# The last stage of a two-layer network kernel: time and scale operands built from x columns with one-hot row factors instead of gathered and transposed rows

## Chip, cores and metric

One Trainium2 chip, one of its cores, one program. The metric is the device time of one execution in microseconds (us), the median of the runs shown. Engines are named as in the profile: PE (TensorE), PEld (its weight loads), DVE (VectorE), ACT (ScalarE), POOL (GpSimd), SP (SyncE, here a queue for DMAs).

## What is computed

Only the last part of the reference matters here. `x` is what the attention half and its MLP leave (4 x 1024 tokens, 512 channels), called x1 below. All in fp32:

```
h = ln(x, pw_g[pathway_ids], pw_b[pathway_ids]);  h = ln(h, cp_g[compartment_ids], cp_b[compartment_ids])
t = ln(x, tm_g[time_steps], tm_b[time_steps])
m, n, r = x + one vector per batch each
s = ln(x, ms_g[scale_type], ms_b[scale_type])
cat = concat([w0*h, w1*t, w2*m, w3*n, w4*r, w5*s])
u = ln(silu(cat @ int_W1 + b1) @ int_W2 + b2, int_g, int_be)
q = round and clip u to int8 by its row maximum;  y = (q @ rhs_q) * scales;  out = x + y
```

The layer norm of `t` and `s` is the same for both: x-hat = (x - mean) * rstd per token. Only the gain row differs: one of 5 for `t`, one of 3 for `s`.

## The kernel before

The program runs an attention half, an MLP half and then this last stage, `conditioned_ffn`. The stage works in 8 blocks (b = 0 to 7) of 512 tokens (BT). A block has 16 steps (NS): four for x (all of m, n, r folded into one weight), four for h, and then t and s in turn, one step for each 128 channels (k = 0 to 3): t0, s0, t1, s1 and so on are steps 8 to 15. `main(b, s)` is 12 PE matmuls of 128x512 (four output tiles by three passes, high and low fp32r parts) into the banks A[0..3]; the last four steps are `main_last`, tile by tile (L2112). Then the second layer, `second` (L2133, 48 matmuls), needs the hidden parts: ACT makes silu and the high part (`hidden`, L2361 and L2364), DVE the low part (L2717). The quantised product of the block before, `ff` (L2060), lies between steps 10 and 13.

An operand of a step is made so: its 128 channels by 512 tokens stand as columns in a PSUM bank, ACT copies them as the high part (`front_high`, L2293) and DVE subtracts that for the low part (`front_low`, L2711). For x the columns are loaded from `x1T_d` into `xs` in SBUF. For h, t and s the rows (128 tokens by 512 channels) are turned by four fp32 PE transposes to a bank (`emit`, L2048).

The rows of t and s: POOL gathers a row of 2 x 512 gains for each token (`gather_ts`, L2537, four indirect DMAs a block), DVE multiplies the time half by x-hat (`t_product`, L2701) and POOL the scale half (`scale_rows`, L2544). x-hat in rows is made by ACT from `x1t` (L2302), with scales that DVE and POOL derive from bn_stats (`x_moments`, `rsqrt`, L2548 and L2550).

Nothing is scheduled by a planner. Each engine has a hand-written order, and semaphores between them. `order` is PE's: before `main` of an even step two "items" (turnings) for the steps two ahead, each in one of four ring banks that its predecessor must have left free. In block 0 `first_order` and DVE's `first_steps` take the place, because weights are still being split (`split_low`, `split_second`) and rhs quantised (`rhs_maximum`, `rhs_peak`, `rhs_multiply`, L2992).

POOL's order in a block b (`body`): `scale_rows(b)`, two gathers of h rows for b + 1, the scales of u of block b - 1 (`rsqrt(US)`, L2548), `tail_gain` (eight operations, L2579 and L2581), the scales of x and then the h rows of b + 1 (`tokens`: L2557, L2559, and the gathers L2518 and L2528), the scales of h (`rsqrt(HS)`, ending with L2550), `tail_add` of two tiles (L2587), `gather_ts(b + 1)`, `tail_add` of the other two. ACT's order after step 15 is: h_centre of b + 1 for two tiles, which waits for the scales of h, and only then `hidden(b)`.

SP's order (`tail`): residual loads, for each q tile a DMA transpose (`turn`), the load of x1 rows two blocks ahead, then the stores of the output.

Of the kernel before, what the change touches and what calls it, by code (L numbers as in the profile page):

```python
# [95 lines left out]
def adaln_attn_ffn_kernel(nc, ins, out):  # L96
# [5 lines left out]
    x1T_d = nc.dram_tensor("x1T_d", (D, TOK), F32, kind="Internal").ap().rearrange("(k p) t -> p k t", p=P)  # L102

    ctx = ExitStack()
    with ctx:
# [17 lines left out]
        def following(sems, marks):  # L123
            return mlp_half(nc, at, sems, marks, ps, vec, v, ident, ones_r, eps6, ins, xT, hs2_d, x1_d, x1T_d, p_d, out_v)
# [718 lines left out]
def mlp_half(nc, at, sems, att, ps, vec, v, ident, ones_r, eps6, ins, xT, hs2_d, x1_d, x1T_d, p_d, out_v):  # L843
# [87 lines left out]
    ffn = conditioned_ffn(nc, at, cleared, ps, vec, v, ident, ones_r, ins, x1_d, x1T_d, xt, out_v)  # L931
# [750 lines left out]
def conditioned_ffn(nc, at, cleared, ps, vec, v, ident, ones_r, ins, x1_d, x1T_d, xt, out_v):  # L1682
# [55 lines left out]
    sT = small("states_sb", [P, KT, GROUP])  # L1738
    sel = small("group_sum", [P, GROUP])
# [7 lines left out]
    rstd = small("rstds", [P, 3, TT])  # L1747
    sc = small("token_scale", [P, 3, TT])
    shift = small("mean_shift", [P, 3, TT])
# [35 lines left out]
    cp_rows, ts_rows = sem("f_cp_rows"), sem("f_time_scale_rows")  # L1785
# [39 lines left out]
    T_AT = 0  # L1825
    QT_AT, FF_AT = 8, 10
    QT_STEP = [9, 9, 10, 11]
    ABS_AT, W2_AT, PEAK_AT = 5, 8, QT_AT
    PEAK = {0: 1, 2: 2, 3: 3}

    items = []

    def add_items(s):
        o, k = steps[s]
        items.append((FRONT[o], k, ("op_low", NS, s, 0)))

    order = []
    for s in range(NS):
        if s % 2 == 0 and XF <= s + AHEAD < NS:
# [12 lines left out]
    for n in (0, 4):  # L1852
        at_main = next(i for i, x in enumerate(first_order) if x == ("item", n)) + 2
        first_order.insert(at_main - 2, first_order.pop(at_main))
# [8 lines left out]
    FREED = {2: 1, 3: 2, 6: 3, 7: 4}  # L1863

# [9 lines left out]
    def sync_program(sp, mlp):  # L1874
# [9 lines left out]
        def tail(b, nxt2):  # L1884
# [15 lines left out]
            for t in range(1, TT):  # L1900
                turn(t)
# [11 lines left out]
        def body(b, q, nxt, nxt2):  # L1913
            if nxt:
                sp.wait_ge(S["oh_done"], b + 1)
                load_ids(b + 1)
            if isinstance(b, int) and b == 0:
                sp.wait_ge(S["xh_done"], TT * 2)
                load(2)
            else:  # L1920
                tail(b, nxt2)
# [35 lines left out]
        def early():  # L1957
# [4 lines left out]
            for k in range(2, KT):  # L1962
                sp.dma_start(xs_first[:, k - 2], x1T_d[:, k, bass.ts(0, BT)]).then_inc(first_loaded, 16)
            sp.wait_ge(S["xh_done"], TT)
            load(1)
            sp.wait_ge(tab_zero, 1)
            load_ids(0)

# [4 lines left out]
        def prepare():  # L1973
            sp.wait_ge(ts_rows, 16 * TT)
# [6 lines left out]
            sp.wait_ge(S["op_low"], XF)  # L1981
            sp.dma_start(rows[:].rearrange("p r d -> p (r d)"), ins["rows"]).then_inc(ld["rows"], 16)
# [15 lines left out]
    def tensor_program(pe, mlp, bank_at):  # L1998
        def wait_bank(b, n, prev):
# [7 lines left out]
            while m >= 0 and items[m][0] == "qt" and prev:  # L2007
                m -= len(ring)
            while m >= 0 and items[m][0] in ("qt", "ff") and not prev:
                if items[m][0] == "qt" and items[m][1] in PEAK:  # L2010
                    pe.wait_ge(peak_read, PEAK[items[m][1]])
                    return
                m -= len(ring)
# [14 lines left out]
        def item(b, q, n, prev):  # L2028
# [8 lines left out]
            wait_bank(b, n, prev)  # L2037
            emit(b + off, q if off == 0 else 1 - q, n)

        def emit(b, q, n, dst=None):  # L2040
# [3 lines left out]
            if kind in ("th", "tt", "ts"):  # L2044
                pe.wait_ge(S[{"th": "h_prod", "tt": "t_prod", "ts": "s_prod"}[kind]], TT * (b + 1))
                for t in range(TT):
                    src = {"th": hn[:, t], "tt": gts[t][:, 0], "ts": gts[t][:, 1]}[kind]
                    i = pe.transpose(dst[:, t * P:(t + 1) * P], src[:, k * P:(k + 1) * P], ident[:])  # L2048
# [14 lines left out]
        def peak_item(n, src, ready, count):  # L2063
            wait_bank(0, n, False)
# [5 lines left out]
        def main(b, s):  # L2070
            o, k = steps[s]
            if isinstance(b, int) and b == 0:
# [14 lines left out]
            if s == NS // 2:  # L2087
                if isinstance(b, int) and b == 0:
                    pe.wait_ge(tab_done, 1)
                pe.wait_ge(S["oh_done"], b + 1)  # L2090
                for m in range(KT):
                    rows_m = slice(GROUP * m, GROUP * (m + 1))
                    i = pe.matmul(A[m][:], bias_t[rows_m, :], oh[rows_m, :], start=False, stop=False,  # L2093
                                  tile_position=(GROUP * m, 0))
# [45 lines left out]
        def body(b, q, prev, nxt):  # L2140
            for what, n in order if prev else first_order:
                if what == "main":
                    if n < NS - LG:
                        main(b, n)
                elif prev and items[n][0] == "qt":
                    continue
                elif prev or items[n][0] not in ("qt", "ff"):
                    item(b, q, n, prev)
# [43 lines left out]
        def early(j):  # L2192
# [28 lines left out]
            elif j == 8:  # L2221
                pe.wait_ge(c_chain, 6)
                for k in range(KT):
# [11 lines left out]
            elif j == 10:  # L2235
                pe.wait_ge(b16_done, 4)
# [889 lines left out]
```

## Time and profile before

| | |
|---|---|
| median of 3 runs | 1745.47 us (1743.71 to 1745.48) |
| profiled execution, own time | 1745.17 us |
| its span | 1743.3 us |
| PE busy | 1731.6 us (99%) |
| DVE / ACT / POOL busy | 1192.5 / 875.4 / 789.0 us (68 / 50 / 45%) |
| granted PE clock | 0.999 of full speed |
| last stage | from 1209.6 us to the end, a block takes 64 to 66 us |

A busy PE means here that a matmul is in flight; matmuls are pipelined, so 12 of them whose mean duration reads 389 ns follow one another every 0.23 us. What an engine costs is therefore read from the distance of starts. The span is 1.9 us below the execution's own time; both differ from the median by under 0.3 us apart from that.

### The profile page before, as it was taken

To read this page: it belongs to the slowest core of one execution; us is meant where nothing else is said; L and a number is where in the kernel's file an instruction comes from. 1 tells how busy PE (TensorE), PEld (TensorE's weight loads), DVE (VectorE), ACT (ScalarE), POOL (GpSimd) and SP (SyncE) were. 2 spreads that over 40 slices of the span, in tenths; PEclk is the share of its full clock that TensorE was granted. 3 is DMA by queue.
4 is the path that set the end of the run, shared out by engine and by line. 5 is a ranking of instruction groups with operands and counts; after the bars stand their busy time and mean duration, and the time that the engine had idled before them with its cause. 6 is when DMAs were issued, how large, how long until landed. Compare 5 with 4: busy or idle time off the path is not lost. (4 is left out here: it accounts for less than half of the span.)

```text
span 1743.3 us, 23362 instructions
## 1 busy us (share of the span) xinstructions
PE 1731.6 (99%) x7935; PEld 1408.6 (81%) x7935; DVE 1192.5 (68%) x1756; ACT 875.4 (50%) x1299; POOL 789.0 (45%) x702
## 2 busy tenths in 40 slices
PE   9999999999999999999999999999999999999998
PEld 7888888888888888888888888778887787788786
DVE  7766666669989688785563335357886687577565
ACT  7655556565666665674562223243453443443433
POOL 1122221222686566665560000015577877878742
PEclk9999999999999999999999999999999999999999
DMA  6011100120243334222536568877645445544511
GB/s 208 1 49 49 48 21 27 49 73 25 97 142 121 124 103 163 97 97 89 187 136 224 192 199 283 325 253 244 222 138 180 140 161 174 157 158 151 162 47 61
DMA packets 121992, 234.36 MB, mean 134 GB/s; under 512 B 25619, under 2 KB 25875, under 8 KB 121893
## 3 DMA queue, kind: packets, MB, share of 16 engines
q1 hardware_dynamic: 91732, 157.63, 27.1%
q0 software_dynamic: 11776, 41.95, 7.2%
q10 hardware_dynamic: 18384, 33.56, 5.6%
q8 instruction: 50, 0.82, 0.2%
q14 instruction: 50, 0.40, 0.1%
HBM read 170.71 MB, written 58.72 MB: 132 GB/s over the span
## 5 line engine op out<-in xcount | busy, mean ns | idle before, releaser
L1081 PE MATMUL bank<-h_parts,mlp_w 128*128 128x512 f32 x2016 | 459.3, 389 | 0.6 <-ACT product_copy L1301 0.5
L1081 PEld LDWEIGHTS bank<-h_parts,mlp_w 128*128 128x128 f32 x2016 | 378.1, 188 | 80.4 <-ACT product_copy L1301 1.4
L358 PE MATMUL bank<-h_parts,gate_w 128*128 128x512 f32 x1536 | 351.1, 389 | 0.6 <-DVE h_parts L695 0.6
L358 PEld LDWEIGHTS bank<-h_parts,gate_w 128*128 128x128 f32 x1536 | 288.1, 188 | 61.9 <-issue 0.9
L2085 PE MATMUL bank<-operand_parts,int_w 128*128 128x512 f32 x1152 | 279.0, 395 | 0.1
L1146 PE MATMUL bank<-p_parts,mlp_out_w 128*128 128x512 f32 x1152 | 267.4, 391 | 0.0
L1146 PEld LDWEIGHTS bank<-p_parts,mlp_out_w 128*128 128x128 f32 x1152 | 214.7, 188 | 48.0 <-issue 2.5
L2085 PEld LDWEIGHTS bank<-operand_parts,int_w 128*128 128x128 f32 x1152 | 212.5, 188 | 45.5 <-issue 1.7
L620 POOL TENSOR_TENSOR decay_sq<-decay 128x512 f32<-128x512 f32 x32 | 39.2, 1226 | 278.8 <-DVE decay L708 278.8
L1422 POOL TENSOR_TENSOR product_out<-product_out,gelu 128x512 f32<-128x512 f32 x69 | 119.7, 1756 | 96.8 <-DVE product_out L1581 96.2
L1301 ACT ACTIVATE product_copy<-bank,vec_sb 128x512 f32<-128x512 f32 x144 | 99.1, 688 | 106.4 <-PE bank L1081 105.3
L1519 DVE TENSOR_TENSOR p_parts<-p_tile,p_parts 128x512 fp32r<-128x512 f32 x96 | 69.2, 729 | 101.6 <-ACT p_parts L1258 101.6
L1258 ACT ACTIVATE p_parts<-p_tile 128x512 fp32r<-128x512 f32 x96 | 59.7, 630 | 128.9 <-PE bank L1146 109.9
L2548 POOL TENSOR_TENSOR rstds<-rstds,minus_half 128x4 f32<-128x4 f32 x23 | 26.5, 1152 | 185.4 <-DVE mean_shift L2684 184.9
L2293 ACT ACTIVATE operand_parts<-bank 128x512 fp32r<-128x512 f32 x96 | 54.9, 590 | 105.1 <-PE bank L2048 101.5
L2711 DVE TENSOR_TENSOR operand_parts<-bank,operand_parts 128x512 fp32r<-128x512 f32 x96 | 65.3, 684 | 43.3 <-ACT operand_parts L2293 36.7
L2133 PE MATMUL bank<-int_w,hidden_parts 128*128 128x512 f32 x384 | 89.9, 390 | 1.3 <-DVE hidden_parts L2717 0.9
L2112 PE MATMUL bank<-operand_parts,int_w 128*128 128x512 f32 x384 | 90.1, 394 | 0.0
L2133 PEld LDWEIGHTS bank<-int_w,hidden_parts 128*128 128x128 f32 x384 | 71.7, 188 | 18.0 <-issue 2.6
L2112 PEld LDWEIGHTS bank<-operand_parts,int_w 128*128 128x128 f32 x384 | 72.0, 188 | 15.7
L627 POOL TENSOR_TENSOR u<-u,y 128x512 f32<-128x512 f32 x32 | 53.8, 1710 | 59.2 <-DVE u L766 59.2
L1509 DVE TENSOR_TENSOR mlp_w<-raw_mlp_w,mlp_w 128x768 fp32r<-128x768 f32 x42 | 44.3, 1055 | 48.5 <-ACT mlp_w L1234 48.5
(311 smaller groups left out, 2755.8 us busy)
## 6 DMA issues: line engine op xcount, KB each, us to landing
p_tile<-p_d ACTq DMA_DIRECT2D x96, 256.0 KB, 4.9
p_d<-product_out SPq DMA_DIRECT2D x92, 256.0 KB, 2.0
raw_mlp_w<-mlp_gate_g SPq DMA_DIRECT2D x21, 512.0 KB, 3.6
raw_mlp_w<-mlp_fc_g SPq DMA_DIRECT2D x21, 512.0 KB, 4.1
xin<-xT SPq DMA_DIRECT2D x8, 1024.0 KB
hs_d<-u SPq DMA_DIRECT2D x8, 1024.0 KB, 5.0
hs_pair<-hs_d SPq DMA_DIRECT2D x8, 1024.0 KB, 7.6
x_columns<-xT SPq DMA_DIRECT2D x8, 1024.0 KB, 6.7
```

What stands on the lines that cost most here:

```text
L358: i = pe.matmul(bank[:], gw[:, w, s, k, m * P:(m + 1) * P], hr[:, q, t, k, :], start=k == 0 and n == 0, stop=k == KT - 1 and n == 2)
L1081: i = pe.matmul(bank[:], wb[g % 2][:, s, w, kk, :], hop[u % 2][o][:, t, kk, :], start=first and kk == 0 and n == 0, stop=kk == 1 and n == ...
L1146: i = pe.matmul(ACC[b % 2][c][:], ow[j // KT][:, s, j % KT, c * P:(c + 1) * P], pr[n % NPR][:, w, :], start=j == 0 and m == 0, stop=j == F ...
L1258: act.activation(pr[n % NPR][:, 0, :], pt[n % NPT][:], ACT.Copy).then_inc(p_high, 1)
L1301: act.activation(dst[:], src[:], ACT.Identity, bias=v(names[g % 2], 2 * VISITS[g // 2][2] + m)).then_inc(done, 1)
L1422: pool.tensor_tensor(po(i)[t][:], po(i)[t][:], gl[t][:], ALU.mult).then_inc(p_mul, 1)
L1519: dve.tensor_tensor(pr[n % NPR][:, 1, :], pt[n % NPT][:], pr[n % NPR][:, 0, :].bitcast(F32), ALU.subtract).then_inc(p_low, 1)
L2085: i = pe.matmul(A[m][:], w1[OPER[o]][:, a, k, m * P:(m + 1) * P], op[:, s % 4, c, :], start=s == 0 and n == 0, stop=False)
L2112: i = pe.matmul(A[m][:], w1[OPER[o]][:, a, k, m * P:(m + 1) * P], op[:, s % 4, c, :], start=False, stop=s == NS - 1 and n == 2)
L2133: i = pe.matmul(A[t][:], zr[:, a, k, t * P:(t + 1) * P], w2[:, c, k, :], start=k == 0 and n == 0 and not ending, stop=k == KT - 1 and n == 2)
L2293: act.activation(op[:, s % 4, 0, :], bank(kind, k)[:], ACT.Copy).then_inc(S["op_high"], 1)
L2711: dve.tensor_tensor(op[:, s % 4, 1, :], x_columns(b, k) if o == "x" else bank(FRONT[o], k)[:], op[:, s % 4, 0, :].bitcast(F32), ALU.subtra ...
```

## The change

What it does:

- t and s are made in columns. POOL makes x-hat columns `xn` from the x columns `xs` by a multiplication and an addition (`xhat_columns`), with the per-token scale and shift spread over all partitions (`spread`). Where scale_rows stood, it makes k = 2 and 3; where gather_ts stood, k = 0 and 1 of the next block.
- For `spread`, PE turns the 128x8 scales and shifts (`turn_stats`, into the ring bank of the second layer's third quantised item, `qt` 2, unused in steady blocks), ACT copies the 8 rows out (`stats_out`), SP stores them to DRAM (`store_stats`) and loads them back broadcast to all partitions (`load_stats`), around its last `turn`.
- The gain of each token comes from PE: one matmul of 32 rows, the gain table's high and low halves times the one-hot matrix `oh`, into a ring bank, in one of four row groups (`gain_of`). Each replaces four transposes.
- DVE multiplies bank and x-hat (`gain_product`, 8 a block) to `tn` or in place to `xn`, both in SBUF; `front_high` and `front_low` read there for t and s.
- Removed: the four indirect DMAs `gather_ts`, `scale_rows`, `t_product`.
- The items of steps 8 to 11 stand together ahead of step 6, those of 12 to 15 ahead of step 10; the bias matmuls move from after step 8 to before step 10.

```diff
-            for ahead in (AHEAD, AHEAD + 1):
-                add_items(s + ahead)
-                order.append(("item", len(items) - 1))
+    ITEMS_AT = {2: (4, 5), 4: (6, 7), 6: (8, 9, 10, 11), 10: (12, 13, 14, 15)}
+    GAINS_AT = {6: (8, 9), 7: (10, 11), 10: (12, 13), 11: (14, 15)}
+    BIAS_AT = 10
+    FIRST_STAT_QT, FIRST_STAT_AT = 1, 10
+    STAT_QT, STAT_AT = 2, 11
...
+        def store_stats(b):
+            sp.wait_ge(stat_rows_done, b + 1)
+            sp.dma_start(stats_d[b], stat_rows[0:2 * TT, :]).then_inc(stats_stored, 16)
+        def load_stats(b):
+            sp.wait_ge(stats_stored, 16 * (b + 1))
+            if b:
+                sp.wait_ge(xn_add, KT * b)
+            for c in range(2):
+                sp.dma_start(spread[:, c, :], stats_d[b:b + 1, c * TT:(c + 1) * TT]...partition_broadcast(P))
...
-            for t in range(1, TT):
-                turn(t)
+            turn(1)
+            turn(2)
+            if nxt:
+                store_stats(b + 1)
+            turn(3)
+            if nxt:
+                load_stats(b + 1)
...
+        def turn_stats(b, n, prev):
+            wait_bank(b - 1, n, prev, True)
+            pe.wait_ge(S["x_rs"], 2 * (b + 1))
+            pe.transpose(bank_of[n][0:2 * TT, 0:P], rs[:, XS].rearrange("p c t -> p (c t)"), ident[:])
...
+            elif kind in ("tt", "ts"):
+                pe.wait_ge(S["oh_done"], b + 1)
+                group, c = gain_of(kind, k)
+                i = pe.matmul(dst[:], gains[group, c, :], oh[group, :], start=True, stop=True, tile_position=(group.start, 0))
...
+            act.wait_ge(S[{"h": "th_ps", "t": "t_prod", "s": "s_prod"}[o]], KT * b + k + 1)
             act.wait_ge(S["z_ps"], (NS - 1) * b + s - 3)
+            act.activation(op[:, s % 4, 0, :], source(b, s), ACT.Copy).then_inc(S["op_high"], 1)
...
-        def scale_rows(b):
...
-                pool.tensor_tensor(gts[t][:, 1], gts[t][:, 1], xh[:, t, :], ALU.mult).then_inc(S["s_prod"], 1)
+        def xhat_columns(b, k):
...
+            pool.wait_ge(stats_loaded, 32 * (b + 1))
+            pool.tensor_tensor(by_tile(xn[:, k]), by_tile(x_columns(b, k)), spread_of(0), ALU.mult).then_inc(xn_mul, 1)
+            pool.wait_ge(xn_mul, KT * b + k + 1)
+            pool.tensor_tensor(by_tile(xn[:, k]), by_tile(xn[:, k]), spread_of(1), ALU.add).then_inc(xn_add, 1)
...
         def body(b, q, prev, nxt):
             if prev:
-                scale_rows(b)
+                xhat_columns(b, 2)
+                xhat_columns(b, 3)
...
             if nxt:
-                for t in range(TT):
-                    gather_ts(b + 1, t, t == 0)
+                xhat_columns(b + 1, 0)
+                xhat_columns(b + 1, 1)
...
-        def t_product(b, t):
...
+        def gain_product(b, s):
+            o, k = steps[s]
+            dve.wait_ge(S[FRONT[o] + "_ps"], KT * b + k + 1)
+            dve.wait_ge(xn_add, KT * b + k + 1)
+            dve.tensor_tensor(source(b, s), xn[:, k], bank(FRONT[o], k)[:], ALU.mult).then_inc(S[o + "_prod"], 1)
...
         def front_low(b, s):
+            dve.tensor_tensor(op[:, s % 4, 1, :], source(b, s), op[:, s % 4, 0, :].bitcast(F32), ALU.subtract)
```

In `first_steps` the four `t_product` and four `s_product_first`, all ahead of the first wait for turned t columns, are gone; the eight `gain_product` stand later, in pairs ahead of the `front_low` of their steps.

## Rows read from the trace of the kernel before

**Rows 1.** Busy times of all engines in block 4: stretch, length, PE, PEld, DVE, ACT, POOL.

```profile
1469.00:1533.00 64.00, 64.00 (x310) 51.59 (x309) 45.46 (x89) 27.72 (x46) 50.20 (x50) 1.00 0.51 159
```

**Rows 2.** Timeline of PE in block 4: start, length, line, tiles, shape, count.

```profile
1469.17 5.61 PE L2085 MATMUL bank<-operand_parts,int_w 128*128 128x512 f32 x24
...
1487.30 1.04 PE L2048 MATMUL bank<-ident_sb,time_scale_rows 128*128 128x128 f32 x8
1488.09 5.72 PE L2085 MATMUL bank<-operand_parts,int_w 128*128 128x512 f32 x24
...
1494.43 2.98 PE L2085 MATMUL bank<-operand_parts,int_w 128*128 128x512 f32 x12
1497.34 0.51 PE L2093 MATMUL bank<-one_hot,bias_table 32*128 32x512 f32 x4
1497.78 3.02 PE L2085 MATMUL bank<-operand_parts,int_w 128*128 128x512 f32 x12
...
1522.32 11.04 PE L2133 MATMUL bank<-int_w,hidden_parts 128*128 128x512 f32 x48
1533.20 5.61 PE L2085 MATMUL bank<-operand_parts,int_w 128*128 128x512 f32 x24
```

**Rows 3.** Groups by line: the turnings of t and s rows, busy and mean.

```profile
L2048 PE MATMUL bank<-ident_sb,time_scale_rows 128*128 128x128 f32 x256 | 33.1, 272 | 0.0
```

**Rows 4.** Timeline of PE: starts of blocks 1, 2, 3, 7; late second layer.

```profile
1274.79 5.61 PE L2085 MATMUL bank<-operand_parts,int_w 128*128 128x512 f32 x24
...
1330.98 9.77 PE L2133 MATMUL bank<-int_w,hidden_parts 128*128 128x512 f32 x42 [0.30 <-DVE hidden_parts L2717]
1340.59 5.61 PE L2085 MATMUL bank<-operand_parts,int_w 128*128 128x512 f32 x24
...
1405.11 5.61 PE L2085 MATMUL bank<-operand_parts,int_w 128*128 128x512 f32 x24
...
1661.29 5.61 PE L2085 MATMUL bank<-operand_parts,int_w 128*128 128x512 f32 x24
```

**Rows 5.** Timeline of POOL in block 1: the scales of h are ready.

```profile
1324.64 0.20 POOL L2550 TENSOR_TENSOR mean_shift<-mean_shift,rstds 128x4 f32<-128x4 f32 x1
```

**Rows 6.** Timeline of block 4 around the hidden parts, POOL and DVE.

```profile
1516.30 0.20 POOL L2550 TENSOR_TENSOR mean_shift<-mean_shift,rstds 128x4 f32<-128x4 f32 x1
1516.46 2.54 POOL L2587 TENSOR_TENSOR u_tiles<-u_tiles,x_residual 128x512 f32<-128x512 f32 x2
...
1519.33 0.71 DVE L2717 TENSOR_TENSOR hidden_parts<-hidden_full,hidden_parts 128x512 fp32r<-128x512 f32 x1 [5.12 <-ACT hidden_parts L2364]
```

**Rows 7.** DVE and POOL at once; then durations of L2711 (min/median/max ns).

```profile
1478.88 1.30 POOL L2579 TENSOR_TENSOR u_tiles<-u_tiles,int_rows 128x512 f32<-128x512 f32 x1 [0.93 <-ACT u_tiles L2302]
1479.00 1.72 DVE L2701 TENSOR_TENSOR time_scale_rows<-time_scale_rows,xhat 128x512 f32<-128x512 f32 x1
...
1587.96 3.45 DVE L2717 TENSOR_TENSOR hidden_parts<-hidden_full,hidden_parts 128x512 fp32r<-128x512 f32 x1 [1.75 <-ACT hidden_parts L2364]
1588.30 2.56 POOL L2587 TENSOR_TENSOR u_tiles<-u_tiles,x_residual 128x512 f32<-128x512 f32 x2
...
L2711 DVE TENSOR_TENSOR operand_parts<-bank,operand_parts x96: 666/686/694, 1220.1 to 1703.5; 128x512 fp32r<-128x512 f32 x96
L2711 DVE TENSOR_TENSOR operand_parts<-x_columns,operand_parts x30: 676/797/3427, 1204.2 to 1662.8; 128x512 fp32r<-128x512 f32 x30
```

**Rows 8.** Timeline of POOL in block 4: scales of u start, scales of x done.

```profile
1476.21 1.38 POOL L2548 TENSOR_TENSOR rstds<-rstds,minus_half 128x4 f32<-128x4 f32 x1
...
1490.84 0.33 POOL L2550 TENSOR_TENSOR mean_shift<-mean_shift,rstds 128x4 f32<-128x4 f32 x1
```

**Rows 9.** Timeline of block 0: DVE's first low parts of t, rhs, then ACT's hidden.

```profile
1233.65 1.29 DVE L2711 TENSOR_TENSOR operand_parts<-bank,operand_parts 128x512 fp32r<-128x512 f32 x2 [2.51 <-ACT operand_parts L2293]
...
1257.44 2.49 DVE L2992 TENSOR_TENSOR u_tiles<-u_tiles,x_residual 128x512 f32<-128x512 f32 x4
...
1260.50 0.67 ACT L2361 ACTIVATE hidden_full<-bank,vec_sb 128x512 f32<-128x512 f32 x1
```

More of the change, by code:

```diff
@@ L1834, in add_items @@
         o, k = steps[s]
-        items.append((FRONT[o], k, ("op_low", NS, s, 0)))
+        items.append((FRONT[o], k, {"h": ("op_low", NS, s, 0), "t": ("t_prod", KT, k, 0), "s": ("s_prod", KT, k, 0)}[o]))
     order = []
     for s in range(NS):
-        if s % 2 == 0 and XF <= s + AHEAD < NS:
-            for ahead in (AHEAD, AHEAD + 1):
-                add_items(s + ahead)
-                order.append(("item", len(items) - 1))
+        for later in ITEMS_AT.get(s, ()):
+            add_items(later)
+            order.append(("item", len(items) - 1))
         order.append(("main", s))
@@ L1851, in conditioned_ffn @@
     first_order = list(order)
-    for n in (0, 4):
-        at_main = next(i for i, x in enumerate(first_order) if x == ("item", n)) + 2
-        first_order.insert(at_main - 2, first_order.pop(at_main))
+    for n, count in ((0, 2), (4, 4)):
+        at_main = next(i for i, x in enumerate(first_order) if x == ("item", n)) + count
+        first_order.insert(at_main - count, first_order.pop(at_main))
     assert len(items) % len(ring) == 0
@@ L1863, in conditioned_ffn, with gain_of, source @@
     FREED = {2: 1, 3: 2, 6: 3, 7: 4}
+    def gain_of(kind, k):
+        group = (2 * k + (kind == "ts")) % 4
+        return slice(GROUP * group, GROUP * (group + 1)), k // 2
+    def source(b, s):
+        o, k = steps[s]
+        if o == "x":
+            return x_columns(b, k)
+        return {"h": lambda: bank("th", k)[:], "t": lambda: tn[:, k % 2], "s": lambda: xn[:, k]}[o]()
     def item_no(kind, k):
@@ L2071, in main @@
             o, k = steps[s]
+            if s == BIAS_AT:
+                if isinstance(b, int) and b == 0:
+                    pe.wait_ge(tab_done, 1)
+                pe.wait_ge(S["oh_done"], b + 1)
+                for m in range(KT):
+                    rows_m = slice(GROUP * m, GROUP * (m + 1))
+                    pe.matmul(A[m][:], bias_t[rows_m, :], oh[rows_m, :], start=False, stop=False, tile_position=(GROUP * m, 0))
             if isinstance(b, int) and b == 0:
@@ L2086, in main @@
                                   start=s == 0 and n == 0, stop=False)
[L2087 to L2094, printed above, removed]
             i.then_inc(S["z_ps"], 1)
@@ L2317, in u_centre, with stats_out @@
                 centre(US, b, t, ut[:, t, :], ut[:, t, :], "u", "u_norm")
+        def stats_out(b):
+            act.wait_ge(stat_ps, b + 1)
+            if not (isinstance(b, int) and b == 1):
+                act.wait_ge(stats_stored, 16 * b)
+            act.activation(stat_rows[0:2 * TT, :], bank("qt", FIRST_STAT_QT if isinstance(b, int) and b == 1 else STAT_QT)[0:2 * TT, 0:P], ACT.Copy).then_inc(stat_rows_done, 1)
         def q_mul(b, t):
@@ L2385, in body @@
                     split_high(2)
+                if not prev and s == 3:
+                    act.wait_ge(gain_loaded, 16)
+                    act.activation(gain_hi[:], gain_raw[:], ACT.Copy).then_inc(gain_high, 1)
                 if not prev and s == ABS_AT:
@@ L2771, in steps_of @@
                     table_rows_now(b + 1)
-                if T_AT <= s < T_AT + TT:
-                    t_product(b, s - T_AT)
+                for later in GAINS_AT.get(s, ()):
+                    gain_product(b, later)
                 if nxt and X_AT <= s < X_AT + TT:
```

192 lines of the change are left out of this document (118 added, 74 removed).

## Prediction

> **What bounds the kernel now.** I read the busy times by stretch first, then PE's timeline of one block, then who waits for whom around the second layer, and last the pairs of DVE and POOL instructions that run at once. In block 4 PE is in flight for all 64.00 us, DVE 45.46 and POOL 50.20 [rows 1]. So PE ends last, and less PE work should be less time. But the timeline shows how close another chain is. Call H the moment when POOL has the scales of h (L2550). ACT centres h first and then makes the hidden parts, so the second layer hangs on H. In block 1 H is 1324.84, the last 42 matmuls start at 1330.98 behind a DVE wait, and the next block starts at 1340.59, so H + 15.75 [rows 4, 5]. That block takes 65.80 us from start to start, block 2 64.52 [rows 4]. In block 4 H is 1516.50 and the next block starts 16.70 later [rows 2, 6]. There PE decides, with 0.95 us to spare: a faster PE can gain that and no more until H comes earlier. H lies 47.33 us behind the start of block 4: 7.04 to the start of the scales of u, 14.96 to the end of the scales of x, 25.33 from there [rows 2, 6, 8]. This is POOL work nearly throughout, and the change leaves it in place.
>
> **The change on PE.** A pair of items, eight transposes, moves the next matmul by 0.79 us [rows 2]; four pairs a block are 3.2 us (busy 33.1 us for 256 agrees with 4.1 a block, overlapped ends included [rows 3]). The pace of full matmuls is 0.229 us (42 from 1330.98 to 1340.59 [rows 4]), 2.75 for a step; from 1494.43 to 1497.78 there are 3.35, so the four bias matmuls of 32 rows cost 0.60 together [rows 2]. The eight new ones are of this form in the same four row groups: four cost 0.60 ahead of step 6, the others stand beside the bias matmuls, at 0.44 (the start distance of those four [rows 2]). The turned statistics are one transpose, 0.10 by 0.79 / 8. Sum on PE: 3.2 - 1.0 - 0.1 = 2.1 us less a block. If all of it counted, eight blocks would give 17 us.
>
> **Waits on PE.** The turned statistics want the scales of x, ready 22.0 us into the block [rows 2, 8], and PE comes to them after step 10; step 9 starts 28.6 us into the block [rows 2], so they are over 30 us in and nothing is lost. The item of step 11 needs the ring bank of step 7 while it now stands ahead of step 6; before, an item came two steps ahead of its use. DVE makes that low part about when PE arrives. I price it 0 to 1 us, take 0, and say that PE has some 3 us of cover by then if the chain through H decides. The last `turn` now follows the statistics on SP, and the fourth `ff` may wait for it: 0 to 1 us, under the same cover. Behind the turned statistics on PE wait `ff` 0 and the rest of the block, behind the store on SP the last `turn`, behind the load the stores of the output, which wait for POOL anyway.
>
> **DVE.** Eight products from PSUM at 0.69 (the form of L2711 from a bank, 666 to 694 ns over 96 [rows 7]) are 5.5 us, less four `t_product`, 2.7. The low parts of t and s keep their count but lose the bank as a source. That is the point of my argument. With one input in PSUM L2711 never took more than 694 ns, with two in SBUF 676 to 3427 [rows 7]. The reason is in the pairs: POOL's L2579 runs from 1478.88 to 1480.18, DVE's L2701 starts at 1479.00 and ends at 1480.72, 0.54 after POOL [rows 7]. A DVE operation with both inputs in SBUF waits for the POOL operation under way. POOL in turn loses about 0.45 when DVE slips in between (an estimate: DVE's 0.54 less the 0.1 by which starts and ends overlap in these rows).
>
> **The clash behind H.** Now POOL has `tail_add` for 2.54 us from H, and then indirect DMAs, beside which DVE's first low part (2.83 after H) takes 0.71 [rows 6]. After the change the first x-hat multiplication of the next block starts right there, 2.50 after H and 0.33 ahead of DVE; its inputs are long there. Four POOL operations of 1.3 follow without a pause, against DVE's four low parts. Taking turns: POOL to 3.8, DVE to 4.35; POOL to 5.5, DVE to 6.05; POOL to 7.2, DVE to 7.75. PE's last 42 matmuls want the third low part; they start 6.14 after H in block 1 [rows 4, 5], and would start 7.9 after it. So the next block starts at H + 17.5 instead of H + 15.75.
>
> This place has a rule in the Trainium skill, SBUF — State Buffer, section "Who interferes with whom": a DVE instruction with two SBUF inputs and a GpSimd instruction that reads SBUF exclude each other, and the later one waits for the whole of the earlier. One row goes past it: DVE waits from 1587.96 over two POOL operations, 3.45 us [rows 7]. By the rule the price stays as I have it; if DVE lost two turns each time, a block would take 1.3 us more and the sum would be 8 us higher.
>
> **H itself.** The first part, 7.04, ends with two gathers that wait for DVE's idx_now, which stands behind two low parts of x. They now run beside four dependent POOL operations that can't start before the x columns of k = 2, 3 land. Bounds 0 and 1.4 (two operations of 1.3 less one), taken 0.6. The second part loses the meeting with `t_product`: -0.3. The third part, h rows, now meets low parts 13 and 14 with two SBUF inputs: two times 0.45, +0.9, bounds 0 and 2.3 (five low parts). H lies then at 7.6 + 14.7 + 26.2 = 48.5, and a block takes 48.5 + 17.5 = 66.0 us. PE alone would need 62.
>
> **Block 0.** Its last phase is tied to DVE: rhs multiplication starts at 1257.44, ACT's first hidden tile at 1260.50, and the next block at 1274.79, 17.35 after the former [rows 4, 9]. DVE idles 2.51 us before its first low parts of t at 1233.65 [rows 9], because PE gets to those items late. The eight removed products stood before this idle time, the eight new ones stand after it: 8 x 0.61 = 4.9 us are moved from slack into the chain. 0.5 of it is hidden (the first product can start some 0.75 earlier). I take +4.4, bounds 0 and 6.5 (with two clashes).
>
> **Sum.** Block 0 +4.4; block 1 66.0 for 65.8, +0.2; block 2 66.0 for 64.5, +1.5; blocks 3 to 6 264.0 for 256.2 (1405.11 to 1661.29 [rows 4]), +7.8; block 7 has no next block, hence no H and no clash, -2.1. Together +11.8. The profiled execution took 1745.17, 0.3 under the median of the runs shown, so about 1757.0. The MLP half gets one more tiny transpose and copy, under other work, at nothing.
>
> **Rivals.**
> 1. No clash that counts, H where it was (not slower). Deciding point: whether DVE's first low part finds POOL in the x-hat multiplication. If statistics or columns come late, or POOL yields, blocks 3 to 6 gain the 0.95 of block 4 each, blocks 1 and 2 nothing, block 7 2.1, block 0 nothing: 1745.2 - 5.9 = 1739. For it: fewer gathered bytes, so landings may be earlier. Against: 0.33 us of order are the same by construction in each block. 0.16.
> 2. PE decides everywhere, the full 17 us: 1728. It needs no clash and H 1.2 us earlier (15.75 + 47.33 less 61.9). 0.04.
> 3. Only block 0 is late: 1739 + 4.4 = 1743. 0.10.
> 4. Clash without a late block 0: 1757 - 4.4 = 1753. 0.10.
> 5. DVE falls behind altogether, low parts 8 to 15 all blocked and H 2 us further out, or two turns lost each time: 66.0 + 2 for six blocks, 1769 and up. 0.10.
> 6. The transposes don't get cheaper (row groups in series, 0.23 each): PE saves 1.3 instead of 2.1 a block, which changes only block 7, 1758. It goes into the forecast's range.
>
> **How the numbers follow.** The forecast, clash and late block 0, has 0.50: 1757, own range 1751 to 1766 (H from -0.6 to +1.4 in six blocks). Faster by over 0.2% (under 1742, about what a measurement of this kernel can tell) are rivals 1 and 2: 0.20. Within 0.2% (1742 to 1749) rival 3 and some of the low edges: 0.15. Slower the rest: 0.65. For 8 in 10 the range takes in most of rival 1 and the start of rival 5: 1738 to 1770.
>
> **What would show it.** PE: gaps before L2133's third k group in all of blocks 1 to 6, released by DVE's hidden low parts, and those low parts at 1.5 us and more beside the x-hat operations of POOL. From H to the next block 17.5. H 48 to 49 into the block. In block 0 the rhs multiplication near 1262. Between items PE's pace as worked out, 2.1 us less a block, seen in block 7. The prediction is wrong if the hidden low parts still take 0.7, or if H comes earlier than 47 us into a block.

## The result: 1.3% slower, and the profile after

| | before | after |
|---|---|---|
| median | 1745.47 us (1743.71 to 1746.22) | 1767.8 us (1766.06 to 1771.16) |
| ratio, 95% interval | 1 | 1.0132 (1.0114 to 1.015) |
| profiled execution, span | 1743.3 us | 1764.9 us |
| granted PE clock, mean | 0.999 | 0.995 |

The forecast was 1757.0, with an own range of 1751 to 1766 and an 8 in 10 range of 1738 to 1770. The sign and the wide range held, the own range did not; the size was 11 us short. One execution of experiment 4 below took 6164.5 us and is left out of its time and ratio.

The stage block by block, from the start of one first layer to the next (starts of the PE groups of L2158, L2085 before). H is, as in the prediction, the moment when POOL has the scales of h; it is counted from the start of its block, the last column from H. In b0 the next block starts 20.8 behind H (before 17.8).

| kernel | b0 | b1 | b2 | b3 | b4 | b5 | b6 | H, b1 to b6 | next block behind H, b1 to b6 |
|---|---|---|---|---|---|---|---|---|---|
| before | 65.2 | 65.8 | 64.5 | 64.1 | 64.0 | 64.1 | 64.0 | 50.1 to 46.4 | 15.8 to 17.6 |
| after | 74.2 | 66.8 | 70.1 | 68.1 | 66.6 | 66.6 | 64.7 | 49.4, 51.9, 49.7, 49.1, 49.2, 47.2 | 17.4; 18.3, 18.4 in b2, b3 |

Page after, the engines, then in the groups by line the hidden low parts and the second operation of POOL's h rows; the same two groups before stand in the second fence:

```profile
PE 1722.5 (98%) x7743; PEld 1387.3 (79%) x7751; DVE 1251.9 (71%) x1786; ACT 880.5 (50%) x1307; POOL 819.6 (46%) x698
...
L2805 DVE TENSOR_TENSOR hidden_parts<-hidden_full,hidden_parts 128x512 fp32r<-128x512 f32 x32 | 49.0, 1581 | 49.0 <-ACT hidden_parts L2441 49.0
L2648 POOL TENSOR_TENSOR h_norm<-h_norm,pw_rows 128x512 f32<-128x512 f32 x32 | 48.9, 1529 | 2.5
```

```profile
L2717 DVE TENSOR_TENSOR hidden_parts<-hidden_full,hidden_parts 128x512 fp32r<-128x512 f32 x32 | 27.5, 858 | 57.6 <-ACT hidden_parts L2364 54.5 <-issue 3.1
L2559 POOL TENSOR_TENSOR h_norm<-h_norm,pw_rows 128x512 f32<-128x512 f32 x32 | 43.2, 1351 | 2.5
```

PE is in flight 9 us less than before; DVE is busy 59 us more. The low parts take 1.8 times as long as before.

Timeline of block 4 after, POOL, DVE and PE around the second layer (it answers to [rows 6], and its last two PE rows to [rows 2]). L2785 are the h products, DVE's multiplication of h by its second gain rows:

```profile
1536.61 0.20 POOL L2639 TENSOR_TENSOR rstds_and_shifts<-rstds_and_shifts 128x4 f32<-128x4 f32 x1
...
1539.26 1.27 POOL L2631 TENSOR_TENSOR xhat_columns<-x_columns,x_scale_shift 128x512 f32<-128x512 f32 x1
...
1539.64 6.52 DVE L2805 TENSOR_TENSOR hidden_parts<-hidden_full,hidden_parts 128x512 fp32r<-128x512 f32 x4 [7.18 <-ACT hidden_parts L2441]
...
1540.61 1.61 POOL L2633 TENSOR_TENSOR xhat_columns<-xhat_columns,x_scale_shift 128x512 f32<-128x512 f32 x1
...
1542.18 1.72 POOL L2631 TENSOR_TENSOR xhat_columns<-x_columns,x_scale_shift 128x512 f32<-128x512 f32 x1
...
1542.92 0.94 PE L2198 MATMUL bank<-int_w,hidden_parts 128*128 128x512 f32 x3 [0.80 <-DVE hidden_parts L2805]
...
1544.61 9.81 PE L2198 MATMUL bank<-int_w,hidden_parts 128*128 128x512 f32 x42 [0.75 <-DVE hidden_parts L2805]
...
1549.49 3.58 DVE L2785 TENSOR_TENSOR h_norm<-h_norm,cp_rows 128x512 f32<-128x512 f32 x4
...
1551.11 1.41 POOL L2631 TENSOR_TENSOR xhat_columns<-x_columns,x_scale_shift 128x512 f32<-128x512 f32 x1 [2.10 <-DMA x_columns<-x1T_d]
...
1554.25 1.07 PE L2158 MATMUL bank<-operand_parts,int_w 128*128 128x512 f32 x4
```

H is 1536.81. POOL's x-hat operation starts 0.38 ahead of DVE, and from there the two take turns: four low parts in 6.5 us. PE waits twice for a low part and starts its last 42 matmuls 7.8 behind H, the next block 17.44.

PE in block 7, after and then before (no next block, so no chain through H):

```profile
1685.55 5.61 PE L2158 MATMUL bank<-operand_parts,int_w 128*128 128x512 f32 x24
...
1703.76 0.51 PE L2114 MATMUL bank<-one_hot,gain_table 32*128 32x512 f32 x4
1704.20 11.22 PE L2158 MATMUL bank<-operand_parts,int_w 128*128 128x512 f32 x48
1715.34 0.51 PE L2114 MATMUL bank<-one_hot,gain_table 32*128 32x512 f32 x4
1715.68 0.41 PE L2144 MATMUL bank<-one_hot,bias_table 32*128 32x512 f32 x4
1716.01 3.02 PE L2158 MATMUL bank<-operand_parts,int_w 128*128 128x512 f32 x12
...
1736.29 2.21 PE L2198 MATMUL bank<-int_w,hidden_parts 128*128 128x512 f32 x9
```

```profile
1714.70 2.21 PE L2133 MATMUL bank<-int_w,hidden_parts 128*128 128x512 f32 x9
```

50.74 us from the block's start to the second layer, against 1714.70 - 1661.29 = 53.41 ([rows 4] for the start): PE's gain is real, 2.7 us.

Block 0 after, DVE and PE:

```profile
1232.21 0.69 DVE L2791 TENSOR_TENSOR time_columns<-xhat_columns,bank 128x512 f32<-128x512 f32 x1 [3.98 <-PE bank L2114]
...
1244.39 0.49 PE L2114 MATMUL bank<-one_hot,gain_table 32*128 32x512 f32 x1 [2.05 <-DVE rhs_peak L3077]
1247.77 0.79 PE L2114 MATMUL bank<-one_hot,gain_table 32*128 32x512 f32 x1 [2.89 <-ACT stat_rows L2394]
...
1262.33 2.48 DVE L3087 TENSOR_TENSOR u_tiles<-u_tiles,x_residual 128x512 f32<-128x512 f32 x4
...
1282.62 1.66 PE L2158 MATMUL bank<-operand_parts,int_w 128*128 128x512 f32 x6 [0.80 <-DVE u_tiles L2823]
```

And what the prediction had not thought of, the granted clock by stretch (the column before the last two). Up to the last second layer these are the only stretches of the stage below full speed, with the ones that follow them, 1253 (0.86), 1409 (0.69) and 1478 (0.81):

```profile
1247.00:1250.00 3.00, 2.23 (x8) 1.40 (x9) 3.00 (x5) 0.71 (x3) 2.13 (x2) 0.50 0.28 96
1250.00:1253.00 3.00, 3.00 (x9) 2.33 (x8) 3.00 (x4) 0.00 (x0) 1.64 (x2) 0.50 0.88 202
...
1406.00:1409.00 3.00, 2.19 (x6) 1.00 (x4) 3.00 (x3) 2.59 (x5) 2.92 (x3) 0.74 0.34 91
...
1475.00:1478.00 3.00, 2.26 (x5) 1.43 (x6) 3.00 (x3) 2.64 (x5) 2.92 (x2) 0.62 0.07 27
```

0.50 is 1.2 GHz instead of 2.4. Each falls behind gaps of PE: the two of block 0 above, and the gaps in the second layers of blocks 2 and 3, the two of blocks 1 to 6 with more than 17.5 behind H. Blocks 1, 4 and 5 have such gaps too and kept full clock. Missing clock times 3 us, summed over the seven stretches, is 6.8 us of PE's work (an estimate from these rows). Before, no stretch of blocks 0 to 7 up to the last second layer was below 0.98.

### The profile page after: what moved, and what is told of

Same layout as the page of the kernel before. It is cut to its first block and busy times, and to the rows that moved or that the text cites. A ratio compares the mean times of both kernels' runs of the same rounds, so it can differ in the third digit from the quotient of the medians.

```text
span 1764.9 us, 23145 instructions
## 1 busy us (share of the span) xinstructions
PE 1722.5 (98%) x7743; PEld 1387.3 (79%) x7751; DVE 1251.9 (71%) x1786; ACT 880.5 (50%) x1307; POOL 819.6 (46%) x698
## 3 DMA queue, kind: packets, MB, share of 16 engines
q1 hardware_dynamic: 94308, 161.99, 27.6%
## 5 line engine op out<-in xcount | busy, mean ns | idle before, releaser
L2158 PE MATMUL bank<-operand_parts,int_w 128*128 128x512 f32 x1152 | 277.3, 397 | 1.0 <-DVE u_tiles L2823 0.8
L2158 PEld LDWEIGHTS bank<-operand_parts,int_w 128*128 128x128 f32 x1152 | 215.3, 189 | 51.7 <-issue 4.9
L2198 PE MATMUL bank<-int_w,hidden_parts 128*128 128x512 f32 x384 | 96.0, 403 | 17.6 <-DVE hidden_parts L2805 9.7
L2637 POOL TENSOR_TENSOR rstds_and_shifts<-rstds_and_shifts,minus_half 128x4 f32<-128x4 f32 x23 | 25.9, 1127 | 187.5 <-DVE rstds_and_shifts L2773 187.3
L2805 DVE TENSOR_TENSOR hidden_parts<-hidden_full,hidden_parts 128x512 fp32r<-128x512 f32 x32 | 49.0, 1581 | 49.0 <-ACT hidden_parts L2441 49.0
L1411 POOL TENSOR_TENSOR mlp_w_sums<-raw_mlp_w 128x256 f32<-128x256 f32 x42 | 40.7, 970 | 66.1 <-DMA raw_mlp_w<-mlp_gate_g 64.9
```

The lines of the kernel that those rows point to most:

```text
L2158: i = pe.matmul(A[m][:], w1[OPER[o]][:, a, k, m * P:(m + 1) * P], op[:, s % 4, c, :], start=s == 0 and n == 0, stop=False)
L2198: i = pe.matmul(A[t][:], zr[:, a, k, t * P:(t + 1) * P], w2[:, c, k, :], start=k == 0 and n == 0 and not ending, stop=k == KT - 1 and n == 2)
L2805: dve.tensor_tensor(zr[:, 1, m, :], tf[:, m % 2, :], zr[:, 0, m, :].bitcast(F32), ALU.subtract).then_inc(S["z_low"], 1)
```

## Experiments

Each stands against the kernel before on its own chip; the changed kernel is 1.0132 in that measure.

**1. Hold POOL back (e1_xhat_waits).**

```diff
             if nxt:
+                pool.wait_ge(S["z_low"], KT * b + 3)
                 xhat_columns(b + 1, 0)
```

> The changed kernel with one wait more: POOL starts the x-hat columns of the next block only when three of DVE's four hidden low parts are done. My theory (the two engines take turns there, and PE's last 42 matmuls wait for it): the hidden low parts end at 3.5, 4.8 and 6.0 us behind the scales of h instead of 4.3, 6.0 and 7.6, the next block comes 15.8 behind them instead of 17.4, so -1.6 us in each of blocks 1 to 6 and -2.4 in block 0: 1767.8 - 12 = 1756, range 1753 to 1760. Rival A (the wait holds back more than it frees): load_x of k = 2, 3 waits for the x-hat multiplications, so the scales of u start up to 3.5 us later in the next block and H with them: 1768 to 1785. Rival B (the clash only moves on to the h products and take_u): half the gain, about 1762.

1786.6 us, 1.0238 (1.0214 to 1.0263), beyond every range. Block 3, H = 1472.59:

```profile
1478.74 9.77 PE L2198 MATMUL bank<-int_w,hidden_parts 128*128 128x512 f32 x42 [0.30 <-DVE hidden_parts L2806]
...
1480.68 3.47 DVE L2801 TENSOR_TENSOR operand_parts<-x_columns,operand_parts 128x512 fp32r<-128x512 f32 x2
...
1484.07 6.84 DVE L2786 TENSOR_TENSOR h_norm<-h_norm,cp_rows 128x512 f32<-128x512 f32 x4
1485.26 3.43 POOL L2676 TENSOR_TENSOR u_tiles<-u_tiles,x_residual 128x512 f32<-128x512 f32 x2
...
1491.66 1.57 PE L2158 MATMUL bank<-operand_parts,int_w 128*128 128x512 f32 x5 [3.15 <-DVE u_tiles L2824]
```

The low parts came free (third end at 6.0), and the next block came 19.0 behind H. The turns moved on: two x low parts and four h products at 1.7 each, and `take_u` (DVE takes the second layer's result from the bank, L2824), for which PE waits 3.15 us, stands behind them in DVE's order. That is rival B's mechanism, and it cost more than the theory hoped to gain. Rival A's did not come: the scales of u start 6.6 to 7.7 into a block, as in the changed kernel (6.5 to 7.7). The low clock followed too: 17 us by the estimate above, at the start of six of the blocks 1 to 7.

**2. PE's waits ahead of the last `ff` (e2_turn_first).** `turn(3)` ahead of `store_stats(b + 1)`.

> The changed kernel with the fourth turn on SP ahead of the store of the statistics. My theory: PE's waits of 1.2 to 1.8 us ahead of ff 3 in blocks 1 to 5 go, but the chain through the scales of h decides those blocks, so only block 2 (whose second layer PE reached 2.5 us late) gains: -2.5, 1765, range 1762 to 1768. Rival (PE's time counts in every block): -1.7 in five blocks, 1759. Rival (the statistics land later and the x-hat columns with them): slower, up to 1772.

1770.2 us, 1.0149 (1.0131 to 1.0168): no gain. Over blocks 1 to 7 PE's wait for turned q fell from 9.1 to 2.8 us, its waits in the second layer grew from 16.0 to 18.1, in single gaps of up to 2.2, and the low clock cost 13.6 us instead of 6.8 in the profiled runs. Block 2 took 68.0 instead of 70.1 us, about what the theory gave it, but blocks 3, 4 and 6, where the clock fell, came 19.1 to 19.7 behind H. PE's waits ahead of the last `ff`, up to 1.8 us where the prediction had 0 to 1, had cover; what PE saves early, it waits later in one piece.

**3. Block 0 (e3_block0_fill).** In `first_steps`:

```diff
             split_low(*SLOT[1], [1])
+            split_low(*SLOT[2], [1])
+            split_low(*SLOT[1], [2])
+            split_low(*SLOT[2], [2])
             gain_product(0, 8)
```

(removed from where they stood behind `front_low(0, 10)` and `rhs_peak`)

> The changed kernel with three DVE low parts of first-layer weights of block 0 moved from behind rhs_maximum into DVE's idle 4 us ahead of the first gain product. My theory (block 0 ends with DVE's chain, which is full from that product to the rhs multiplication): 3 x 0.74 = 2.2 us less, and the rhs multiplication 2 to 3 us nearer to the start of the block; 1765.5, range 1763.5 to 1767. Rival (PE's waits of 2.0 and 2.9 us for ring banks in block 0 decide, which this doesn't touch): no change, 1767.8.

1765.7 us, 1.0104 (1.0087 to 1.0121). Block 0 took 71.1 us instead of 74.2; the median is 2.1 lower, and the interval still touches that of the changed kernel (1.0114 to 1.015), so the gain is read from block 0 and not from the time. DVE's order binds block 0, and the idle 3.98 us ahead of its first gain product was where time could be had.

**4. More PE work (e4_items_twice).** Each of the eight row-group matmuls of a block is done twice.

> The changed kernel with each of the eight row-group matmuls of a block done twice into the same bank (same result): about 8 x 0.23 = 1.8 us more on PE in a block. My theory (blocks 1 to 6 hang on the scales of h, PE has cover there): only block 7 and perhaps a block whose PE is late pay, +2 to +4: 1770 to 1772. Rival (PE decides in every block): +14, 1782.

1773.5 us, 1.0142 (1.0121 to 1.0162). The experiment was weaker than meant: eight matmuls in four row groups move the next one by 0.68 us where four took 0.44, so a block had 0.47 us more and not 1.8. The rival would have given 8 x 0.47 = 3.8. The ratios overlap, so this run decides nothing.

**5. Take the lock from the hidden parts (e5_hidden_in_bank).** In blocks 0 to 6 ACT writes silu to a PSUM bank, as soon as that is free, and DVE's low part then has one input in SBUF:

```diff
+    def hidden_full(nxt):
+        return [ring[0][:], ring[1][:]] if nxt else [tf[:, 0, :], tf[:, 1, :]]
-                act.activation(tf[:, m % 2, :], A[m][:], ...
+                act.activation(full[m % 2], A[m][:], ...
```

> The changed kernel with ACT's hidden tile written to a free ring bank instead of SBUF (blocks 0 to 6), so that DVE's hidden low parts have one input in PSUM; POOL's x-hat operations stay where they are. My theory (the clash behind the scales of h is one of two SBUF readers): the low parts take 0.7 us beside the x-hat operations, the third ends 6.0 us behind the scales of h instead of 7.6, PE no longer waits between its first groups of the second layer long enough to lose its clock, and no h product is blocked: next block 15.8 behind the scales of h at best, -1.6 in blocks 1 to 6, -2.4 in block 0, and 2 to 4 less for lost clock: about 1752, range 1749 to 1758. Rival A (as in e1, the turns only move on to the x low parts and h products, and take_u is late): 1762 to 1770. Rival B (low parts are slow for another reason than the shared SBUF inputs): still 1.7 us each, 1768.

1761.7 us, 1.0088 (1.0071 to 1.0105). The group of the low parts, then block 3, H = 1464.24:

```profile
L2814 DVE TENSOR_TENSOR hidden_parts<-bank,hidden_parts 128x512 fp32r<-128x512 f32 x28 | 19.4, 692 | 51.4 <-ACT hidden_parts L2449 50.9 <-issue 0.5
```

```profile
1470.21 9.79 PE L2201 MATMUL bank<-int_w,hidden_parts 128*128 128x512 f32 x42 [0.24 <-DVE hidden_parts L2814]
...
1474.12 6.86 DVE L2793 TENSOR_TENSOR h_norm<-h_norm,cp_rows 128x512 f32<-128x512 f32 x4
...
1475.75 1.29 POOL L2639 TENSOR_TENSOR xhat_columns<-x_columns,x_scale_shift 128x512 f32<-128x512 f32 x1 [0.41 <-DMA x_columns<-x1T_d]
1477.12 1.62 POOL L2641 TENSOR_TENSOR xhat_columns<-xhat_columns,x_scale_shift 128x512 f32<-128x512 f32 x1
...
1481.73 1.62 PE L2161 MATMUL bank<-operand_parts,int_w 128*128 128x512 f32 x6 [1.74 <-DVE u_tiles L2832]
```

Rival B falls: 0.69 us each, right beside the x-hat operations. Rival A holds: the next block still comes 17.4 to 17.5 behind H, now behind the h products. In the changed kernel they took 3.58 us (block 4), since POOL's x-hat columns of k = 2 started only 14.3 behind H; with the low parts free these columns start 11.5 behind H and meet all four h products, 6.86 us. What was gained (6 us) lies in blocks 2 and 3 of the profiled execution. Behind H they came 0.9 us earlier each, at full clock (only block 0 lost some, 3.4 us). H of block 2 came 4.5 earlier, and there POOL's wait for a gather of h rows fell from 5.16 to under 1; why is not shown.

**6. Take it from the operands (e6_products_in_bank).** t products, and s of k = 0 and 1, written back to their bank:

```diff
+    def in_bank(o, k):
+        return o == "h" or o == "t" or o == "s" and k < 2
```

> The changed kernel with six of the eight gain products written back into their PSUM bank (t all, s of k = 0, 1), banks released by the low part: six of eight low parts have one input in PSUM again. My theory (the stretch from the scales of x to the scales of h is longer by 2 to 4 us than before because POOL's h rows and gathers meet these low parts): that stretch is 25.5 to 26.5 instead of 27.2 to 29.9, H 1.5 to 2.5 us earlier in blocks 1 to 6: -6 to -12, 1757 to 1762. Rival A (DMA landings of the gathers, not the lock, lengthen it): no change, 1768. Rival B (banks held longer make PE wait): slower than 1768.

1758.1 us, 1.0074 (1.0056 to 1.0093). From the scales of x to H it took 27.2, 27.1, 25.9, 27.0, 25.6, 25.8 us in blocks 1 to 6, in the changed kernel 28.7, 29.9, 27.4, 28.5, 27.2, 25.2 (before 25.5 to 24.5). The second operation of the h rows came down from 1529 ns:

```profile
L2653 POOL TENSOR_TENSOR h_norm<-h_norm,pw_rows 128x512 f32<-128x512 f32 x32 | 44.5, 1391 | 2.5
```

Their first operation rose (1307 to 1361 ns), so the two together gave 2.7 us in all blocks, the issue of the gathers of h rows 3.5 (39.7 to 36.2), and POOL's wait for gathered rows 5.5 (18.5 to 13.0); its wait for x-hat from ACT took 3.5 back (16.4 to 19.9). So the longer stretch is tied to the two SBUF inputs of these low parts, but rival A's landings are the largest part of what came back, and this run doesn't separate the two.

**7. Fill PE's gaps (e7_keep_clock).** Three matmuls into a free bank ahead of the waits for k = 1 and 2 of the second layer.

> The changed kernel with three matmuls without a use into a free bank ahead of the waits for the second and the third hidden low part (blocks 0 to 6), which fill PE's gaps of 0.75 us there. Theory C (PE's gaps in the second layer bring the granted clock to the lower of its levels for some us in one to three blocks of a run, and that time is on the path): no stretch of lower clock around the second layer, mean granted clock 0.997 instead of 0.992 to 0.995; next block 17.4 behind the scales of h in every block: -3 to -8, 1760 to 1765. Rival (the lower clock is not on the path, or comes from elsewhere): unchanged, 1767 to 1769.

1763.2 us, 1.0093 (1.0077 to 1.011). Timeline of PE at the end of block 2 (L2192 are the added ones), and a stretch of that second layer by clock:

```profile
1406.89 0.93 PE L2201 MATMUL bank<-int_w,hidden_parts 128*128 128x512 f32 x3 [1.32 <-ACT hidden_parts L2444]
1407.66 0.86 PE L2192 MATMUL bank<-int_w,hidden_parts 128*128 128x512 f32 x3
1408.62 0.93 PE L2201 MATMUL bank<-int_w,hidden_parts 128*128 128x512 f32 x3
```

```profile
1410.00:1413.00 3.00, 2.93 (x14) 2.25 (x13) 3.00 (x3) 2.39 (x4) 3.00 (x3) 1.00 0.02 5
```

All stretches around second layers were at full clock (block 0 lost 3.4 us as before), blocks 2 and 3 took 66.7 and 66.4, and blocks 1 to 6 came 17.4 to 17.5 behind H. The median is 4.6 us lower, and the intervals don't meet; the mean clock of the four executions was 0.996 to 0.998 instead of 0.992 to 0.995. That much of it is clock is likely but not shown to the full: in the profiled executions 1.8 us came back behind H in blocks 2 and 3, where the clock had fallen, and 3.4 ahead of H in the same blocks, 2.6 of them in block 2, where POOL's wait for a gather was 2.59 us instead of 5.16.

**8. The clash in the kernel before (b1_pool_reads, b2_pool_memsets).** Ahead of the gathers of time and scale rows, four times:

```diff
+                        pool.tensor_tensor(gts[c][:, 0], gts[c][:, 0], gts[c][:, 1], ALU.mult)
```

and in the second kernel `pool.memset(gts[c][:], 0.0)` in its place. The rows are overwritten by the gather.

> The kernel before with four POOL multiplications of SBUF rows (128x512, result overwritten by the gather that follows) ahead of the time and scale gathers, where the changed kernel has its x-hat operations. My theory (that alone makes the clash): hidden low parts of 1.4 to 1.8 us ending 4.3, 6.0, 7.6 behind the scales of h, next block 17.4 behind them in each block, periods +1.7 in block 1 and +0.8 in block 4, and the gathers 5.2 us later, which blocks 1 to 6 may feel at the start of the next block (up to +1): 1752 to 1765. Rival (the changed kernel's low parts are slow for a reason of its own, such as its DMAs): low parts 0.7 us, 1746.

> The kernel before with four POOL memsets of SBUF rows (128x1024, nothing read) in the place where the run before had four multiplications that read SBUF. Theory (reading operands from SBUF makes the turns, not POOL being busy): DVE's hidden low parts 0.7 us beside the memsets, third one 6.0 behind the scales of h. Rival (any POOL operation beside them blocks): 1.4 to 1.8 us again. The time depends on how much later the gathers start: 1746 to 1765.

1787.7 us, 1.0235 (1.0216 to 1.0255), and 1766.0 us, 1.0115 (1.0095 to 1.0134). The hidden low parts in both:

```profile
L2725 DVE TENSOR_TENSOR hidden_parts<-hidden_full,hidden_parts 128x512 fp32r<-128x512 f32 x32 | 50.9, 1638 | 45.5 <-ACT hidden_parts L2364 44.9 <-issue 0.5
```

```profile
L2725 DVE TENSOR_TENSOR hidden_parts<-hidden_full,hidden_parts 128x512 fp32r<-128x512 f32 x32 | 22.1, 692 | 58.2 <-ACT hidden_parts L2364 57.6 <-issue 0.5
```

Four reading POOL operations alone make the clash in the old kernel, with the next block 17.6 behind H (19.2 in block 2); four that only write leave 0.69 and 15.8. The times are worse than I said because the gathers start later and the scales of u with them (10.8 to 12.8 us into a block in the second kernel, before 6.9 to 10.0). In both kernels H of blocks 1 to 6 comes 21 to 22 us later in all; the reading kernel adds 8.0 behind H, 7.5 in block 0 and 3.5 in block 7.

**9. The second victim (e8_late_columns).** Experiment 5, and

```diff
             if prev:
+                pool.wait_ge(S["h_prod"], TT * (b + 1))
                 xhat_columns(b, 2)
```

> The kernel with the hidden tile in a bank, and one wait more: POOL starts the x-hat columns of k = 2 only when DVE's four h products are done. There the low parts were unblocked (third one 5.8 us behind the scales of h) and the next block still came 17.4 behind them, since the two x low parts and four h products took turns with POOL (1.8 us each) and take_u stood behind them. My theory (that second row of turns is what took the gain): h products of 0.7 us, PE without a gap of 2.1 us at the start of a block, next block 15.7 behind the scales of h, scales of u no later than before: 1761.7 - 7 x 1.7 = 1750, range 1747 to 1755. Rival (POOL has no room and starts the scales of u later by as much): 1760 to 1764.

1752.3 us, 1.0039 (1.0025 to 1.0052). H = 1524.45:

```profile
1534.32 3.58 DVE L2794 TENSOR_TENSOR h_norm<-h_norm,cp_rows 128x512 f32<-128x512 f32 x4
...
1538.25 1.30 POOL L2639 TENSOR_TENSOR xhat_columns<-x_columns,x_scale_shift 128x512 f32<-128x512 f32 x1 [2.71 <-DVE h_norm L2794]
...
1540.06 1.75 PE L2161 MATMUL bank<-operand_parts,int_w 128*128 128x512 f32 x7
```

The next block is 15.6 behind H in all six blocks, and block 0 takes 71.2 instead of the 73.8 of experiment 5. The scales of u start at 7.6 to 7.9 instead of 6.4 to 6.6, which gives back some.

**10. Together (e9_together).** Experiments 5, 6, 3 and the wait of 9.

> All that helped, together: hidden tile in a bank, six gain products in their banks, x-hat columns of k = 2, 3 behind the h products, three weight low parts of block 0 in DVE's idle time. My theory (the change itself saves 2 us of PE a block, and what it lost is the turns of DVE and POOL, block 0's full DVE and the clock that fell in the gaps): scales of h 47 us into a block and the next block 15.7 behind them, 62.5 to 63.5 a block in 1 to 6, block 0 4 over the kernel before, block 7 2 under it: 1738, range 1734 to 1746, so faster than both. Rival (PE's waits for banks held longer, or POOL's late start, eat it): 1746 to 1755.

1740.3 us, 0.9965 (0.9953 to 0.9978): faster than the changed kernel by 1.6% and than the kernel before by 0.35%. Blocks 0 to 6 take 69.1, 63.0, 65.5, 63.5, 63.4, 63.3, 62.3. Block 4, H = 1518.24:

```profile
1524.21 9.79 PE L2206 MATMUL bank<-int_w,hidden_parts 128*128 128x512 f32 x42 [0.26 <-DVE hidden_parts L2820]
...
1533.83 1.52 PE L2166 MATMUL bank<-operand_parts,int_w 128*128 128x512 f32 x6
```

Block 2 is open. It takes 2 us more than its neighbours, and POOL waits there 4.05 us for a gather of h rows (in the changed kernel 5.16, before 1.88). Its row in the changed kernel:

```profile
1388.29 1.27 POOL L2646 TENSOR_TENSOR h_norm<-xhat,pw_rows 128x512 f32<-128x512 f32 x1 [5.16 <-DMA pw_rows<-pw_gb,idx_now]
```

The statistics and the last `turn` don't make it late. SP issues them at 1389.62 and 1389.95, behind this landing, and in the combined kernel at 1380.29 and 1380.62, behind the landing at 1378.57. Two earlier turns were under way together with the gather: ACT's wait for one ends at the same 1388.29 and PE's at 1388.35. Whether they hold the gather up, and why in this block, no run shows.

## Why the prediction was right in sign and short in size

**The clash behind H: right, to 0.1 us.** In blocks 1 to 6 the low parts end 4.3, 6.0 and 7.6 to 7.7 behind H, and in blocks 1, 4, 5 and 6 the next block starts 17.4 to 17.5 behind it (predicted 4.35, 6.05, 7.75 and 17.5). Experiments 5 and 8 show the cause: two inputs in SBUF on DVE against a read from SBUF on POOL. The Trainium skill, SBUF — State Buffer, section "Who interferes with whom", says just this, a POOL instruction that only writes excepted; the memsets agree (0.69 us). With its rule that the later one waits for the whole of the earlier the steady turns of 1.7 us here agree, as in the sum; the 3.45 of [rows 7] goes past it and did not come back behind H.

**What stood behind it: outside the sum, and no part of the miss.** The sum asked which DVE operation meets POOL first, and not what else DVE does with two SBUF inputs until `take_u`. In the changed kernel this cost nothing: in blocks 1 to 6 at most one of the four h products was blocked, and PE never waited for `take_u`. It was the theories of experiments 1 and 5 that failed by it. Freed low parts only brought POOL's next reads beside all four h products, and the next block came 19.0 or again 17.4 behind H; with both rows free (9) it came 1.8 us earlier in each block.

**PE: 2.7 us a block and not 2.1.** The eight new matmuls and the bias move the rest by 0.44, 0.34 and 0.33 = 1.1; the sum had 1.6 (the bias at its old 0.60) [rows 2]. Block 7 kept it, as predicted; in blocks 1 to 6 the chain through H took it. Rival 6 is out: two matmuls in each of four row groups take 0.68.

**H: the third part was mis-sized.** The first part came at 6.5 to 7.7 (7.6 predicted). From the scales of x to H it was 27.2 to 29.9 in blocks 1 to 5 where I had 26.2 and a bound of 27.6. I counted two meetings of low parts with h rows. In block 4, 3.1 us longer than before, three of four L2648 took 1.6 us instead of 1.3 and the two gathers beside low parts 1.53 and 1.43 instead of 1.07 and 1.00; POOL also waited 0.75 longer for x-hat and 0.49 longer for a gathered row. Experiment 6 took 1.4 to 2.8 us back in these five blocks. My bound was too narrow because it counted the blocked POOL operations alone, and neither the gathers' issue on the same engine nor these waits. In block 2 the late gather adds 3.3, and its cause is open.

**Block 0: +8.9 and not +4.4.** The step worked out was right: the rhs multiplication starts at 1262.33 (predicted 1262), and filling DVE's idle time gave 3.1 back. I then added 17.35 as in the kernel before. But between the two lie hidden parts and h products that meet POOL, and it took 20.3, which is 2.9 more. The prediction had the clash in its sum for the other blocks and left it out of this one. An earlier start of the stage is 1.1, and the rest of the difference is 0.5.

**The clock: not in the sum.** I priced PE's waits by their length under cover. They also cost clock: the time fell by 4.6 us when experiment 7 filled two of them. Of that the extra 0.8 and 1.0 us of blocks 2 and 3 behind H is shown to be clock. The spread of the runs goes with it (1766 to 1771 at a mean of 0.995 to 0.992).

**The rivals.** No clash (1) and PE everywhere (2) fell with the first row of block 4; block 0 alone (3) and the clash alone (4) each had one half of what came. Rival 5, H 2 us further out and blocks of 68 us, was what blocks 2 and 3 came near to in length (70.1 and 68.1), though only in block 2 by its H, and its 1769 is nearer than my 1757; it named the right place (low parts blocked all along) for part of it.

**By block** the forecast missed 4.5 in block 0, 4.1 in block 2, 2.1 in block 3, 2 in blocks 1, 4 and 5 together, and had 3 too much in block 6, block 7 and the start: 9.7, the distance of the profiled execution (1766.7) from 1757. So the sum came as near as it did in part by luck: errors of 12.7 one way and 3 the other.

## What to carry to other kernels

When work moves from PE or DMA to POOL, list every DVE operation with both inputs in SBUF between the new POOL operations and the next thing that PE waits for, not only the first; here each that met a POOL read took 1.7 us instead of 0.7. Holding POOL back alone made it worse. What helped was place: a bank that is free at that time takes one of DVE's inputs out of SBUF. With that for the hidden parts and six products, one wait and three moved operations, the same change turned from 1.3% slower to 0.35% faster. And a short wait on PE that seems covered can cost a second time, if the clock falls behind it.

## What the runs showed of the hardware

- ACT writes silu to PSUM as fast as to SBUF (0.66 and 0.68 us for 128x512, experiment 5 and the changed kernel), and copies from there in 598 ns instead of 631.
- The four row groups overlap: four matmuls of 32 rows move the next by 0.34 to 0.44 us, eight by 0.57 to 0.68, where twelve full ones take 2.75.
- In the changed kernel each second layer of blocks 1 to 5 has a gap on PE of 1.2 to 1.6 us and then shorter ones of up to 0.8. The granted clock fell to 0.50 behind them in blocks 2 and 3 and stayed at 1.00 in blocks 1, 4 and 5; with the shorter gaps filled and the longer one left (experiment 7) it stayed at 1.00 in all of them.
